# The three bf16 parts of the biases: made by VectorE in the second part of the first layer instead of by GpSimd in its first tiles

## What is computed

```python
h = jnp.maximum(_layernorm(x, axis=-1), 0.0)
x = x + _L0_gnn_ref(h, adj, L0_gnn_W, L0_gnn_b)
...
def _L0_gnn_ref(x, adj, W, b):
    h = adj @ x
    h = h @ W.T + b
    return jax.nn.relu(h)
```

## Time and profile before

| | us |
|---|---|
| median of 3 runs (lowest, highest) | 1038.21 (1037.59, 1038.72) |
| the profiled execution, its own time | 1037.51 |
| its span on the core | 1035.80 |
| PE, DVE, ACT, POOL busy in the span | 978.2, 853.7, 753.8, 300.4 |

### The profile page before, as it was taken

One profiled execution on the slowest core, in us unless ns is written; L12 is line 12 of the kernel. 1 busy time (PEld: TensorE's weight loads), 2 busy tenths in 40 slices (PEclk: granted clock), 3 DMA queues, 4 the chain that ended last, 5 costly groups with the idle time before them and its releaser, 6 DMA issues.

```text
span 1035.8 us, 16367 instructions
## 1 busy us (share of the span) xinstructions
PE 978.2 (94%) x6151; PEld 467.7 (45%) x6151; DVE 853.7 (82%) x1108; ACT 753.8 (73%) x800; POOL 300.4 (29%) x140
## 2 busy tenths in 40 slices
PE   6999979999999999999989998999999999998798
PEld 2444344444544444335444443444554454333455
DVE  6999969898678778799769987878878978898873
ACT  4555545566567666786698899988888888997683
POOL 1069980000000000005025373443333434342001
PEclk9999999999999999999999999999999999999999
DMA  9989997897277787788754445556555553446662
GB/s 340 420 315 422 423 389 242 319 316 271 92 244 251 249 291 268 261 275 281 264 180 152 133 142 170 175 165 192 172 163 163 182 172 114 144 142 212 205 214 83
DMA packets 96349, 238.43 MB, mean 230 GB/s; under 512 B 16400, under 2 KB 45072, under 8 KB 79888
## 3 DMA queue, kind: packets, MB, share of 16 engines
q1 hardware_dynamic: 87056, 220.62, 62.3%
q10 hardware_dynamic: 9216, 16.78, 4.2%
HBM read 219.55 MB, written 17.83 MB: 229 GB/s over the span
## 4 chain that ended last, share of the span: by engine, by line
PE 66%; DVE 18%; ACT 9%; issue 6%; DMA 1%; SPq 0%; DVEq 0%; ACTq 0%
PE PS L592 45%; PE PS L793 7%; PE PS L890 4%; PE PS L921 4%; DVE work L1844 3%; ACT work L1330 2%; ACT work L1338 2%; DVE work L2174 2%; DVE work L2162 1%; ACT work L1341 1%; DVE ring L2180 1%; DVE work L2168 1%; PE PS L604 1%; PE PS L625 1%; ACT work L1324 1%
## 5 line engine op out<-in xcount | busy, mean ns | idle before, releaser
L1239 ACT ACTIVATE work<-PS,att_sc 128x1024 f32<-128x1024 f32 x128 | 149.2, 1202 | 73.3 <-PE PS L793 51.0
L570 POOL TENSOR_TENSOR ring<-work,ring 128x1024 f32<-128x1024 f32 x57 | 135.9, 2384 | 228.3 <-DVE work L2174 228.3
L592 PE MATMUL PS<-ring,work 128*65 128x256 f32 (+1 forms) x600 | 190.8, 466 | 3.9 <-DVE work L2201 3.8
L1152 ACT ACTIVATE work<-PS 128x1024 uint8<-128x1024 f32 x128 | 124.2, 1024 | 93.7 <-PE PS L592 93.3
L1844 DVE TENSOR_TENSOR work<-work,ring 128x1024 f32<-128x1024 f32 x128 | 153.3, 1230 | 45.7 <-ACT work L1239 45.6
L2168 DVE SCALAR_TENSOR_TENSOR work<-PS,work 128x1024 f32<-128x1024 f32 x72 | 88.1, 1223 | 55.1 <-PE PS L592 46.6
L592 PEld LDWEIGHTS PS<-ring,work 128*65 128x65 f32 x600 | 80.4, 138 | 90.9 <-issue 65.5
L1330 ACT ACTIVATE work<-work 128x1024 f32<-128x1024 f32 x72 | 75.9, 1055 | 34.3 <-DVE work L2162 34.2
L592 PE MATMUL PS<-work 128*64 128x512 f32 (+2 forms) x544 | 90.4, 483 | 2.5 <-DVE work L1844 1.2
L2174 DVE SCALAR_TENSOR_TENSOR work<-work 128x1024 f32<-128x1024 f32 x72 | 87.9, 1220 | 2.5 <-ACT work L1345 1.9
L508 POOL CAST bcut<-bias 128x384 bf16<-128x384 f32 x1 | 86.6, 86632 | 0.1
(11 more groups left out here) (304 smaller groups left out, 1490.1 us busy)
## 6 DMA issues: line engine op xcount, KB each, us to landing
ring<-in_adj_t SPq DMA_DIRECT2D x96, 1024.0 KB, 5.5
ring<-in_adj_t SPq DMA_DIRECT2D x104, 512.0 KB, 4.2
work<-in_adj_t SPq DMA_DIRECT2D x32, 1024.0 KB, 9.5
codes<-work ACTq DMA_DIRECT2D x64, 256.0 KB, 7.2
ring<-codes SPq DMA_DIRECT2D x64, 256.0 KB, 4.5
H<-in_adj_t SPq DMA_DIRECT2D x24, 512.0 KB, 4.5
X<-in_x SPq DMA_DIRECT2D x2, 256.0 KB, 4.9
X<-in_x SPq DMA_DIRECT2D x1, 512.0 KB, 10.2
```

Source lines behind the costliest of these rows:

```text
L570: nc.gpsimd.tensor_tensor(near(n), sums(n), near(n), ALU.mult).then_inc(sem("near_ready"), 1)
L592: return mm(out_ap, lhsT, rhs, start=starts, stop=True, skip_group_check=True)
L1152: nc.scalar.activation(made[:, k, u:HALF:2], PS[:, (4 + 2 * u) * BANK:(6 + 2 * u) * BANK], ACT.Relu).then_inc(sem("codes_made"), 1)
L1239: nc.scalar.activation(att[:, u, :], PS[:, (4 + 2 * u) * BANK:(6 + 2 * u) * BANK], ACT.Sigmoid, bias=att_sc[:, 2:3], scale=att_sc[:, 1:2]) ...
```

## The change

GpSimd's function `bias_piece` and the loop that calls it are gone. The same eight operations stand in DVE's `points0`, behind DVE's work on tiles 0 to 3 of the second part: memset and first cast at i = 0, first subtraction and second cast at i = 1, second subtraction at i = 2, and the three copies into `brow` at i = 3. PE's three waits at i = 5 are as before.

```diff
-            def bias_piece(n):
-                if n == 0:
-                    pool.wait_ge(sem("biases_loaded"), 16 * 7)
-                    link(nc.gpsimd.memset(brow[:, :, :], 0.0))
...
-            for n in range(8):
-                pool.wait_ge(sem("agg0_done"), 2 * n + 1)
-                bias_piece(n)
...
             def points0(i):
 
+                if i == 0:
+                    dve.wait_ge(sem("biases_loaded"), 16 * 7)
+                    link(V.memset(brow[:, :, :], 0.0))
+                    link(V.tensor_copy(bcut[0][:, :, :], bias[:, :, :]))
+                if i == 1:
+                    link(V.tensor_tensor(brem[:, :, :], bias[:, :, :], bcut[0][:, :, :], ALU.subtract))
+                    link(V.tensor_copy(bcut[1][:, :, :], brem[:, :, :]))
+                if i == 2:
+                    link(V.tensor_tensor(bcut[2][:, :, :], brem[:, :, :], bcut[1][:, :, :], ALU.subtract))
+                if i == 3:
+                    for k in range(3):
+                        V.tensor_copy(brow[32 * k:32 * k + 1, :, :], bcut[k][32 * k:32 * k + 1, :, :]).then_inc(sem("brow_ready"), 1)
                 if i == 7:
```

## The result

The changed kernel took 1031.47 us (median of 20 runs, 1029.64 to 1038.29). The kernel before, run 20 times beside it, took 1039.97 us (1032.27 to 1043.10). The ratio is 0.9931, 95% interval 0.9914 to 0.9949: **faster by 0.69%**, that is by 7.2 us on 1039.97 (5.3 to 8.9). This is the ratio of the means (1032.73 and 1039.88); the medians are 8.50 us apart, which the interval holds as well. The forecast was 8.72 us less, a ratio of 1029.5 / 1038.21 = 0.9916, which also lies inside, so these runs show no shortfall of the gain. Its time of 1029.5 us doesn't fare as well: the median is 1.97 us above it, and 0.9931 of 1039.97 is 1032.8, 0.6 above the upper end of the range, mostly because the kernel before stands 1.8 us higher than the three runs that I had started from.

A forecast was written before the change was run, and what follows sets the result against it. The prediction took PE's chain as the bound, with a stop for `brow` at i = 5. The wait of 5.73 us and the low clock's 2.99 made 8.72; 1038.21 - 8.72 = 1029.5 us, range 1028.2 to 1032.2.

The forecast's parts named there:

- The wait and its cause: Before the bias matmul at i = 5, PE waits 5.73 us for `brow`, held by GpSimd's cast until VectorE stops.
- The rival in which PE waits for something else: PE's wait at i = 5 was not for `brow` and stays: no change, 1038.2 us, chance 0.03.
- 8.72 us in that place: From tile 5's last count group to tile 6's first, PE would take 4.62 us instead of 13.34.
- Its second part, 2.99 us for the low clock: Linear map and first half of tile 6 ran at TensorE's lower clock after the wait; removing it gains 2.99 us.
- The eight operations: Moved to VectorE, they would cost it 3.3 us, bounds 1.4 and 5.9, and delay PE nowhere.
- the nearest need: The first place where PE would need VectorE's delayed work: the transposition at i = 13, at 175.78 us.
- The free amount: The eight operations on VectorE cost PE nothing up to 4.4 us in all.
- The two rivals that needed costlier operations: VectorE becomes the bound, 1031.0 us, chance 0.08; or far costlier small operations make it slower, 1041.1 us, chance 0.03.
- the sum's last step: From profiled execution, 1028.8 us, to median of runs, 0.70 higher: 1029.5 us, with runs differing by 1.1 us.
- the low clock at 0.06: Rival: the low clock returns at one of PE's short stops ending layer 0, costing 2.99 us: 1032.5 us, chance 0.06.
- the last sign that I had named: The prediction would be wrong if the stages after the change's place are longer than before.

The follow-up runs named there:

- run 20: Not a label but part of "run 20 times beside it": the unchanged kernel before, measured 20 times beside the changed one, median 1039.97 us.
- the filled kernels: Twelve matmuls that nothing reads put into PE's pauses at the end of layer 0: changed kernel 1030.93 us, ratio 0.9905; kernel before 1038.86 us, 0.9989.
- e11_sum_fill: Kernel before, with one sum on VectorE behind tile 0 of the second part and 12 unread matmuls in PE's pauses ending layer 0: 1030.89 us, 0.9907.
- e3_warm: Kernel before, with PE's wait for `brow` filled with 24 matmuls that nothing reads: 1039.81 us, ratio 0.9986.
- e8_before_fill: Kernel before, with 12 matmuls that nothing reads in PE's pauses at the end of layer 0: 1038.86 us, ratio 0.9989.
- e2_stop: Kernel before, with VectorE made to wait for GpSimd's `brow` at tile 0 of the second part: 1033.65 us, ratio 0.9932.
- e6_reduce: Kernel before, with one unused sum on VectorE behind tile 0 and one behind tile 2 of the second part: 1031.29 us, one run.
- e9_one_sum: Kernel before, with a single unused sum on VectorE behind tile 0 of the second part: 1032.28 us, ratio 0.9925.
- e10_one_add: Kernel before, with one unused two-input addition on VectorE behind tile 0 of the second part: 1032.50 us, one run.

## Why the prediction was right or wrong

**The wait and its cause: right.** PE waited for `brow`, `brow` for GpSimd's cast, the cast for a pause of VectorE. The kernel with the stop and the two with a sum show it without the change: GpSimd keeps all its work, and the middle stage falls from 13.34 to 4.62. The cast waits for `agg0_done` and `pool_chain` alone, neither of which VectorE sets: so these two engines meet at more than semaphores, other than the first section says. The rival in which PE waits for something else is dead. The rule of the Trainium skill behind that rival (SBUF — State Buffer, "Who interferes with whom": one instruction holds the shared pair to its end) gave a turn within 2.3 us; measured are 86.63 us over some 50 instructions. The same section says that a `tensor_reduce` on this chip never contends with GpSimd, and there the trace agrees: the cast ends 0.45 us into the sum, at 124.48.

**8.72 us in that place: right**, to the hundredth, in every kernel where `brow` came in time. Its second part, 2.99 us for the low clock, was measured by itself as 2.92.

**The eight operations: right in size**, 3.17 us for 3.3, and free as said: 98.95 us from tile 6 to tile 31 in both kernels. `update0` starts at 150.68 (forecast 150.2). The transposition stands at 176.79, forecast 175.78, later by 1.01, of which the start is 0.93, with no wait, 1.8 us behind the end of the features at 174.98. **Wrong was the nearest need**: I followed VectorE's chain to the features and took tile 8's mask as the only one to look at. Tile 9's, behind `update0` and two steps of the normalization, came first in the doubled kernel. The free amount came out about right (4.8 for 4.4) for the wrong reason. The two rivals that needed costlier operations are out: none of the eight rows is over 0.55 us, and the three copies take 0.80 together.

**What failed is the sum's last step, the level and its spread.** "The median of the runs is 0.70 above that one" and "the runs differ by 1.1 us among themselves" rested on three runs. Twenty runs of before spread over 10.8 us, with a median of 1039.97 us, 1.76 above the 1038.21 of the three; twenty of after spread over 8.7. The level is thus 1.76 of the 1.97 us by which the median missed the forecast, and the range of 4.0 us was built on a spread eight to ten times too small. All three runs lie on the low side, and chance can do that: of the 55 runs of before beside the experiments, the 17 with a mean granted clock of 0.983 or less took 1041.46 us or more, the other 38 took 1041.66 or less.

**With it failed the reason for leaving the low clock at 0.06**: "nothing that PE does there changes but the moment". The end of layer 0 is a stage whose clock isn't fixed by its work. It runs from 15.56 to 21.08 us in the unfilled profiled executions, in kernels with and without the eight operations, and the 21.08 belong to a run of 1036.25 us at a mean clock of 0.983. With the twelve matmuls it takes 15.69 or 15.70 in four executions; all 30 runs of the filled kernels have a mean clock of 0.985 or more, and the twelve of the changed one spread over 5.4 us. So this stage makes a part of the spread, in both kernels: on one chip 17 unfilled runs of before reach up to 1045.41 us and the 12 filled ones up to 1040.99. How large a part is not measured. The range ended at 1032.2, below the 1032.5 that I had given to this rival.

**The gain: 8.72 us stands within what the runs can tell**, 7.2 us by the ratio (5.3 to 8.9) and 8.50 by the medians. The profiled pair gained 6.2 us only, and by the last sign that I had named, a later stage longer than before, the prediction is wrong there. Two terms were missing from the sum for one pair of executions:

- *The start*, 0.93 us. I had no term for it, and none could be read from before. It follows the landing of a load; whether the change has a part in it stays open.
- *The end of layer 0*, 17.10 us against before's 15.56, 1.54 us. It repeats for the same program (17.19), but the changed kernel with its operations doubled takes 15.57 and the kernel before, with edits elsewhere, 16.96 to 21.08. So it is not shown to be a price of the change.

Between the two filled kernels the gain is 7.9 us by the medians, 8.7 by the ratios and 9.2 by the spans of the profiled pair, whose starts are 0.43 apart. So the runs don't tell 8.72 from 8.72 - 0.93 = 7.8.

One more cause is argued and not shown: before had one run at 1032.27 among 20, with the next at 1036.52, and such single runs at about 1030 also stand among its 23 and 17 runs beside the experiments and among the 12 of the filled one (1030.74). A late load that lets GpSimd through, as traced in `e11_sum_fill`, would make them; none of these runs has a trace.

**A version that may beat both** follows from it: the end of layer 0 filled, with the operations on VectorE or with one sum in front of GpSimd's. These gave 0.9905 to 0.991, and moving the operations isn't needed for it. That they beat the changed kernel (0.9931) is not shown.

## What to carry to other kernels

Read the end of a long instruction on one engine against the pauses of its neighbour: where GpSimd's record ends 0.36 us after VectorE's, its length is VectorE's stream, and one sum of 0.69 us or a break of 0.03 us in that stream can be worth the same as moving the work. Price a stop of TensorE with the stretch at the low clock behind it, and look at every later place with short pauses before calling the clock unchanged there. Take the width of a range from more than three runs, or widen it by what the least certain stage of the profile can do.

## What the runs showed that I had not expected

An unbroken stream of masks, degree sums and copies on VectorE kept out one GpSimd cast of 384 numbers a partition, for 86.63 us in before and for 64.55 to 65.49 where something opened. The time from VectorE letting go to the cast's end is the same in all eight traces in which GpSimd has the cast: six stand here, and `e3_warm` and `e8_before_fill`, which end like before, have 0.37 and 0.35.

| | VectorE's last such instruction ends | the cast ends | us between | what follows on VectorE |
|---|---|---|---|---|
| before | 146.86 | 147.23 | 0.37 | wait for PE |
| `e2_stop` | 124.34 | 124.70 | 0.36 | wait for GpSimd |
| `e6_reduce` | 124.12 | 124.48 | 0.36 | a sum |
| `e9_one_sum` | 125.40 | 125.77 | 0.37 | a sum |
| `e10_one_add` | 125.76 | 126.11 | 0.35 | a mask, 0.03 us later |
| `e11_sum_fill` | 67.61 | 67.97 | 0.36 | wait for a load |

GpSimd's memset right in front of the cast, which only writes, took 0.42 us in the same stream. Which of the masks, degree sums and copies keeps the cast out by itself was not tested; an addition with two inputs did, in `e10_one_add`. That a break of 0.03 us is enough rests on the one trace of `e10_one_add`.
